# Column term by GpSimd, row terms moved into the feed-forward, and a new order of loads in a cross-attention and feed-forward kernel

## The chip, the cores and the metric

The kernel runs on one core of one Trainium2 chip. The metric is device time in microseconds. Each of the five engines (TensorE for matmuls, VectorE, ScalarE, GpSimd, SyncE) runs its own queue of instructions in order; they wait for each other by semaphores.
## The reference

```python
# x (2, 1024, 2048), ctx (2, 2048, 2048), kernel (2048, 2048), all float32
def fake_quant(x, scale, zp):
    q = jnp.clip(jnp.round(x / scale + zp), 0, 255)
    return (q - zp) * scale

def _layernorm(x): return (x - mean(x)) / sqrt(var(x) + 1e-5)

x = x + fake_quant(_layernorm(x), s1, z1) @ fake_quant(ctx, s2, z2)

y = _layernorm(x)
base = y @ kernel + bias
# the 2 x 1024 tokens are seen as 8 groups of 256; gate (8, 16)
A_eff = einsum('bn,nri->bri', gate, lora_A)      # rank 32
B_eff = einsum('bn,nor->bor', gate, lora_B)
delta = B_eff @ (A_eff @ y) + lora_B_shared @ (lora_A_shared @ y)
x = x + base + delta
```

## The kernel before

A batch (`b` = 0, 1) has 1024 tokens in 8 tiles of 128 (`TILES`) and 2048 columns in 4 blocks of 512 (`NBLK`). For each batch the attention product runs block by block (`first_by_tile`, blocks `j` = 0 to 3), then the feed-forward, again in 4 blocks. Each block's tile `t` has its own PSUM bank `t`. The inner dimension comes in 4 groups `g` (`NG`) of 4 x 128 rows, held in `ring`.

**Attention.** Both operands are quantised to integers. The product uses integers less 127, which are exact in bf16. With q the integer less 127, and d1, d2 the distances of 127 from the zero points, the result is s1*s2*(q1 q2 + d2*sum(q1) + d1*sum(q2) + constant). The part with sum(q1) is the *row term*: one number per token, `RC`. The part with sum(q2) is the *column term*: one number per column, the same for all tokens. TensorE sums each column with one matmul per block into bank 7 (`column_sum`, bank `CB`); ScalarE and VectorE split it into a high and a low half (`column`, `column_low`), and TensorE adds it to each tile with one more matmul (`column_term`, line 1021). The row term is added to x by ScalarE (`row_term`, line 884). `evict1` (VectorE, line 1409) then adds the scaled product to x, which sits in `x2`; it frees the bank for the next block.

Context groups are loaded to `stage`, converted by ScalarE (`conv_ctx`, line 736) and clipped by VectorE (`ctx_group`, line 1362), which also sums them for the column sum (`add_group`).

**Start of batch 0.** x arrives tile by tile (GpSimd's queue); VectorE makes statistics, GpSimd the inverse roots (`root_pair`), ScalarE the quantised rows (`relu_rows`), VectorE the rounding (`round1`). Tiles 0 to 3 are transposed by TensorE (`turn`, `turn_out`), tiles 4 to 7 by DMA (`turn_q`). After block 0 of batch 0, TensorE forms the gated LoRA matrices (`a_effective`, line 1049; `b_effective`, line 1060) from `lora_a`, `lora_b`; they are written out by `store_a_part` and the stores to `bg_scratch`. Their largest values are found with all-reduces over partitions on GpSimd (`largest`, line 588): 1 for A, 2 for B, 3 and 4 for parts of W.

**Feed-forward.** `norm2` normalises a tile; ScalarE takes the high f16 part (`split_hi`), VectorE the low one (`low2`); SyncE transposes each by DMA (`turn_y`, lines 355 and 360). W is split alike (`conv_w` on ScalarE, line 748; `w_group` on VectorE, line 1396). Each step is three matmuls, high by high, high by low, low by high (lines 1154 to 1156). The first block opens with tiles 0 and 1 together (`base0_pair`): group by group, both tiles. LoRA products follow between the tiles (`lora_in`, line 1177; `product_p`). GpSimd adds the bias to x (`add_bias`, line 617), and `evict2` (line 1448) finishes a tile.

The order on each engine is written out by hand; nothing is rearranged by a scheduler.

## Time and profile before

| | us |
|---|---|
| Median of 3 runs | 1066.53 (1066.3 to 1067.35) |
| Profiled execution, its own time | 1063.74 |
| Profiled execution, span from first to last instruction | 1061.7 |
| TensorE busy | 1003.1 (94%), 4791 matmuls |
| VectorE busy | 532.3 (50%) |
| ScalarE busy | 311.5 (29%) |
| GpSimd busy | 163.4 (15%) |
| TensorE's mean granted clock | 0.989 of full |

A busy share says how long an engine computed, not whether anybody waited for it. In rows of the timeline the first number is the start in us, the second the time in us, then engine, line, operation, written tile, read tiles, shape and count; in square brackets stands how long the engine had been idle before it, and what ended that. Engines are written PE (TensorE), DVE (VectorE), ACT (ScalarE), POOL (GpSimd); SPq and POOLq are instructions of the sequencer. Matmul times overlap (a matmul of 0.38 us follows the last one after 0.22 us), so distances are read from starts.

### The profile page before, as it was taken

How to read it: one execution, taken by the hardware profiler on the slowest of the kernel's cores; microseconds unless marked ns; L12 is line 12 of the kernel's file. 1: busy time of each engine (PE TensorE's matmuls, PEld its weight loads, DVE VectorE, ACT ScalarE, POOL GpSimd, SP SyncE). 2: the span in 40 equal slices, each digit the busy share in tenths (PEclk: the TensorE clock that was granted, in tenths of full speed). 3: DMA queues.
4: the chain of work that ended last, by engine and by line, in shares of the span. 5: the costliest groups of instructions: out<-in, count | busy, mean ns of one | idle time of the engine just before them, and what ended most of it. 6: DMA issues, size and time to landing. Idle time of an engine off the chain costs nothing.

```text
span 1061.7 us, 12294 instructions
## 1 busy us (share of the span) xinstructions
PE 1003.1 (94%) x4791; PEld 472.9 (45%) x4791; DVE 532.3 (50%) x764; ACT 311.5 (29%) x266; POOL 163.4 (15%) x199
## 2 busy tenths in 40 slices
PE   2778999799999999999999999999999999999996
PEld 1345444355544444444444444445544444444442
DVE  6754677879655455463423555987632023014010
ACT  4666731322032132232223743532121021003000
POOL 3101100101102211311510000020104004004110
PEclk9989999899999999999999999999999999999998
DMA  8869682767735446338599844456935025004010
GB/s 365 255 192 368 260 346 96 184 139 183 201 127 195 168 149 212 138 112 251 204 299 262 336 179 159 80 166 147 222 110 169 20 80 187 20 30 158 10 42 27
DMA packets 124392, 181.70 MB, mean 171 GB/s; under 512 B 96064, under 2 KB 96064, under 8 KB 111808
## 3 DMA queue, kind: packets, MB, share of 16 engines
q1 hardware_dynamic: 109600, 118.25, 37.3%
q0 software_dynamic: 13600, 58.73, 15.3%
q10 hardware_dynamic: 1152, 4.19, 1.0%
q8 instruction: 25, 0.41, 0.2%
q14 instruction: 15, 0.12, 0.0%
HBM read 128.72 MB, written 29.36 MB: 149 GB/s over the span
## 4 chain that ended last, share of the span: by engine, by line
PE 68%; DVE 11%; DMA 10%; issue 4%; ACT 3%; POOL 1%; SPq 1%; DVEq 0%; POOLq 0%; ACTq 0%
PE psum L1154 16%; PE psum L1156 16%; PE psum L1155 16%; PE psum L987 15%; DMA stage<-in_w 2%; DMA x<-in_x 2%; PE psum L1177 2%; DMA lhs<-in_lora_b 1%; DVE ring L1396 1%; DMA xn<-in_x 1%; DVE stats L1421 1%; DVE hl L1441 1%; DVE stats L1308 1%; DMA bias_sb<-in_bias 1%; DMA lhs<-ap_st 1%
## 5 line engine op out<-in xcount | busy, mean ns | idle before, releaser
L1154 PE MATMUL psum<-ring,lhs 128*128 128x512 f16 x1024 | 388.8, 380 | 9.4 <-DMA lhs<-hl 7.4
L1155 PE MATMUL psum<-ring,lhs 128*128 128x512 f16 x1024 | 388.8, 380 | 0.0
L1156 PE MATMUL psum<-ring,lhs 128*128 128x512 f16 x1024 | 388.8, 380 | 0.0
L987 PE MATMUL psum<-ring,lhs 128*128 128x512 bf16 x1024 | 235.2, 386 | 9.0 <-DMA lhs<-ap_st 7.1
L987 PEld LDWEIGHTS psum<-ring,lhs 128*128 128x128 bf16 x1024 | 101.4, 99 | 134.8 <-issue 15.4
L1154 PEld LDWEIGHTS psum<-ring,lhs 128*128 128x128 f16 x1024 | 100.3, 98 | 132.3 <-issue 10.1
L1156 PEld LDWEIGHTS psum<-ring,lhs 128*128 128x128 f16 x1024 | 100.4, 98 | 121.3 <-issue 0.8
L1155 PEld LDWEIGHTS psum<-ring,lhs 128*128 128x128 f16 x1024 | 100.3, 98 | 119.9 <-issue 0.8
L1448 DVE SCALAR_TENSOR_TENSOR x<-psum,sc,x 128x512 f32<-128x512 f32 (+1 forms) x64 | 45.3, 746 | 182.2 <-PE psum L1166 181.4
L748 ACT ACTIVATE ring<-stage,sc 128x2048 f16<-128x2048 f32 x32 | 63.7, 2002 | 202.6 <-PE psum L1156 159.4
L617 POOL TENSOR_TENSOR x<-x,bias_sb 128x512 f32<-128x512 f32 (+1 forms) x64 | 87.7, 1396 | 173.5 <-DVE xn L1431 98.2
L1396 DVE SCALAR_TENSOR_TENSOR ring<-stage,sc,ring 128x2048 f16<-128x2048 f32 x32 | 75.7, 2376 | 76.4 <-ACT ring L748 76.2
L736 ACT ACTIVATE ring<-stage,pats_sb,sc 128x2048 int16<-128x2048 f32 x30 | 62.3, 2092 | 75.4 <-DMA stage<-in_ctx_in 37.8
L623 POOL DMA_DIRECT2D out<-x x48 | 26.7, 556 | 241.6 <-DVE x L1448 237.8
L1409 DVE SCALAR_TENSOR_TENSOR x<-psum,sc,x 128x512 f32<-128x512 f32 x64 | 45.6, 746 | 34.8 <-PE psum L1021 33.7
L724 ACT ACTIVATE hl<-xn 128x2048 f16<-128x2048 f32 x16 | 30.6, 1912 | 67.6 <-DVE xn L1431 63.0
L1362 DVE TENSOR_SCALAR ring<-ring 128x2048 bf16<-128x2048 int16 x30 | 20.7, 691 | 58.4 <-ACT ring L736 58.4
L1402 DVE SCALAR_TENSOR_TENSOR b_st<-stage,sc,b_st 64x1024 f16<-64x1024 f32 x16 | 21.6, 1350 | 47.9 <-ACT b_st L755 47.8
L1281 DVE BATCH_NORM_STATS2 stats<-xn 128x6 f32<-128x512 f32 x32 | 19.8, 682 | 47.2 <-DMA xn<-in_x 47.1
L1441 DVE TENSOR_TENSOR hl<-xn,hl 128x2048 f16<-128x2048 f32 x16 | 36.7, 2292 | 4.6 <-DMA lhs<-hl 4.4
L884 ACT ACTIVATE x<-x,sc 128x512 f32<-128x512 f32 (+1 forms) x48 | 37.2, 855 | 0.4 <-DVE sc L1350 0.4
L755 ACT ACTIVATE b_st<-stage,sc 128x1024 f16<-128x1024 f32 x16 | 18.4, 1150 | 63.8 <-DMA stage<-in_lora_bs 63.8
(158 smaller groups left out, 644.9 us busy)
## 6 DMA issues: line engine op xcount, KB each, us to landing
stage<-in_w SPq DMA_DIRECT2D x38, 1024.0 KB, 6.0
stage<-in_ctx_in SPq DMA_DIRECT2D x30, 1024.0 KB, 7.9
out<-x POOLq DMA_DIRECT2D x64, 256.0 KB, 3.5
x<-in_x POOLq DMA_DIRECT2D x8, 1024.0 KB, 11.9
xn<-in_x POOLq DMA_DIRECT2D x8, 1024.0 KB, 7.3
x<-in_x POOLq DMA_DIRECT2D x4, 2048.0 KB, 15.9
lhs<-in_lora_a POOLq DMA_DIRECT2D x4, 1024.0 KB, 6.9
lhs<-in_lora_b SPq DMA_DIRECT2D x4, 1024.0 KB, 13.3
```

The lines of the kernel that those rows point to most:

```text
L617: pool.tensor_tensor(v, v, bias_sb[:, :], ALU.add).then_inc(biased, 1)
L736: act.activation(ring_i[:, g, j % 2, :, :], stage[:, i % 2, :, :], ACT.Relu, bias=Z2, scale=IS2).then_inc(act_conv, 1)
L748: act.activation(ring[:, g, 0, :, :], stage[:, i % 2, :, :], ACT.Copy, scale=of_block(CW0, j)).then_inc(act_conv, 1)
L884: act.activation(v, v, ACT.Identity, bias=RC[:, t:t + 1]).then_inc(with_row, 1)
L987: last = pe.matmul(psum[:, t, :], lhs_q[:, k, t * P:(t + 1) * P], ring_q[:, g, j % 2, u, :], start=(k == 0), stop=False)
L1154: pe.matmul(psum[:, t, :], hi, ring[:, g, 0, u, :], start=(kk == 0), stop=False)
L1155: pe.matmul(psum[:, t, :], hi, ring[:, g, 1, u, :], start=False, stop=False)
L1156: last = pe.matmul(psum[:, t, :], lo, ring[:, g, 0, u, :], start=False, stop=False)
L1396: dve.scalar_tensor_tensor(out=ring[:, g, 1, :, :], in0=stage[:, half_w(b, g), :, :], scalar=of_block(CW0, j), in1=ring[:, g, 0, :, :], op ...
L1409: dve.scalar_tensor_tensor(out=v, in0=psum[:, t, :], scalar=S12, in1=v, op0=ALU.mult, op1=ALU.add).then_inc(evicted, 1)
L1441: dve.tensor_tensor(hl[:, 1, :], xn[:, :], hl[:, 0, :], ALU.subtract).then_inc(y_lo, 1)
L1448: dve.scalar_tensor_tensor(out=v, in0=psum[:, t, :], scalar=of_block(INVS0, j), in1=v, op0=ALU.mult, op1=ALU.add).then_inc(evicted, 1)
```

## The change

It has six parts.

1. **Column term.** Block 0 of batch 0 stays as it was. From block 1 on, ScalarE writes the whole column term in f32 to `bias_sb` (`column`, semaphore `col_row`), GpSimd adds it to each tile of x (`add_column`, semaphore `with_col`), `evict1` waits for `with_col`, and TensorE's `column_term` and VectorE's `column_low` are gone from these blocks. The adds stand in GpSimd's queue between the all-reduces and the stores of A.
2. **Row terms.** They leave the attention blocks; ScalarE adds them to a whole tile (2048 columns) in the feed-forward, after the tile has been normalised. A number that is the same over a token's row drops out of its layernorm.
3. **x.** Tiles 4 to 7 are requested together, and LoRA A parts 0 and 1 right after `root_pair(1)`.
4. **Loads on SyncE.** The first two context groups of block 1 follow the transposes of tiles 4 to 7; LoRA B part 1 comes ahead of context group 2, part 3 ahead of group 3; the context of block 2 waits for `be_full` 8.
5. **Orders on VectorE and ScalarE** at the start (rounding of tiles 4 and 5 and their scales earlier), around the LoRA parts (block 0's evictions before `row_terms`, B's copies apart from their maxima), and in the opening of the feed-forward (`w_group(b, 0, 0)` ahead of tile 2's statistics and of `low2(b, 1)`).
6. **Opening.** `base0_pair` starts with tile 0's first group, then takes the high half of tile 1, and asks for tile 1's low half only later.

```diff
@@ gpsimd
-            load_x([4, 5])
+            load_x(range(4, TILES))
             root_pair(1)
-            load_x([6, 7])
...
+            load_lora_a(0)
+            load_lora_a(1)
             root_pair(2)
-            load_lora_a(0)
             root_pair(3)
-            load_lora_a(1)
...
+            def add_column(b, j, tiles=range(TILES)):
+                pool.wait_ge(col_row, b * NBLK + j)
+                if b:
+                    pool.wait_ge(res_in[j], 16)
+                for t in tiles:
+                    if b == 0:
+                        pool.wait_ge(relued, t + 1)
+                    v = x2[:, t, j * NW:(j + 1) * NW]
+                    pool.tensor_tensor(v, v, bias_sb[:, :], ALU.add).then_inc(with_col, 1)
...
                     largest(1, MX_A, PW_A)
+                    add_column(b, 1, range(2))
                     largest(2, MX_B, PW_B)
-                    store_a(b)
-                    largest(3, MX_W, PW_W)
+                    add_column(b, 1, range(2, TILES))
                 else:
                     load_residual(b, NBLK - 1)
-                    store_a(b)
+                    add_column(b, 0)
+                    add_column(b, 1)
+                store_a(b, [0, 1])
+                add_column(b, 2)
+                store_a(b, [2, 3])
+                add_column(b, 3, [0])
+                if b == 0:
+                    largest(3, MX_W, PW_W)
+                add_column(b, 3, range(1, TILES))
                 add_bias(b, 0, blk2(b, 0), False)
@@ sync
             load_ctx(0, 0, [0, 1])
-            load_ctx(0, 1, [0, 1])
             for t in range(PT, TILES):
                 turn_q(t)
+            load_ctx(0, 1, [0, 1])
...
             load_lora_b(0)
+            load_lora_b(1)
             load_ctx(0, 1, [2])
-            load_lora_b(1)
-            load_ctx(0, 1, [3])
             load_lora_b(2)
             load_lora_b(3)
+            load_ctx(0, 1, [3])
+            sp.wait_ge(be_full, 8)
             load_ctx(0, 2, [0, 1])
...
                         turn_y(b, 0)
-                        turn_y(b, 1)
+                        turn_high(b, 1)
+                    if g == 2 and isinstance(j, int) and j == 0:
+                        turn_low(b, 1)
@@ scalar
+                    if n == 0:
+                        act.activation(col_parts, psum[:, CB, :], ACT.Copy, scale=D1).then_inc(col_hi, 1)
+                    else:
+                        if n > 1:
+                            act.wait_ge(with_col, (n - 1) * TILES)
+                        act.activation(bias_sb[:, :], psum[:, CB, :], ACT.Copy, scale=D1F).then_inc(col_row, 1)
+                def row_term(t):
+                    act.wait_ge(rows_ready, b + 1)
+                    act.activation(x2[:, t, :], x2[:, t, :], ACT.Identity, bias=RC[:, t:t + 1]).then_inc(with_row, 1)
@@ vector
             def evict1(b, j, t):
                 dve.wait_ge(psum_full, blk(b, 0, j) * TILES + t + 1)
-                dve.wait_ge(with_row, (2 + j) * TILES + t + 1 if b else min(j, 1) * TILES + t + 1)
+                if b or j:
+                    dve.wait_ge(with_col, (b * NBLK + j - 1) * TILES + t + 1)
...
                 evict1(b, j, 3)
-                early_stats2(b, 2)
-                late_stats2(b, 2)
+                w_group(b, 0, 0)
                 low2(b, 1)
                 evict1(b, j, 4)
                 evict1(b, j, 5)
-                w_group(b, 0, 0)
                 w_group(b, 0, 1)
                 evict1(b, j, 6)
                 evict1(b, j, 7)
                 w_group(b, 0, 2)
+                stats2(b, 2)
                 w_group(b, 0, 3)
@@ tensor, base0_pair
+                    tile_in(0)
+                    bank_free(k, 0)
+                    pe.wait_ge(converted, grp_w(b, 0, 0) + 1)
+                    base_group(0, 0)
+                    high_in(1)
+                    bank_free(k, 1)
+                    high_group(1, 0)
+                    pe.wait_ge(converted, grp_w(b, 0, 1) + 1)
+                    base_group(0, 1)
+                    low_in(1)
+                    low_group(1, 0)
+                    base_group(1, 1)
```

GpSimd's queue in batch 0, from the stores of the LoRA B parts to the first bias add, before. A row of these lists has the line, the operation, written and read tiles, and the semaphores it waits for; the all-reduces are the rows `ISA sc<-sc`, and a bare `ISA` ahead of them or of an add is a MODIFY_POOL_CONFIG.

```order
L634 DMA bg_scratch<-hl 128x2x512 [waits be_dve,be_act] x2
L588 ISA
L588 ISA sc<-sc 128x1 [waits red_in] x2
L600 DMA a_scratch<-lhs 128x2048 [waits a_lo] x4
L588 ISA sc<-sc 128x1 [waits red_in]
L610 DMA bias_sb<-in_bias 128x512 [waits psum_full]
L617 ISA
L617 TENSOR_TENSOR x<-x,bias_sb 128x512 [waits normed2,bias_in]
```

The same queue after, up to the end of block 1's adds:

```order
L656 DMA bg_scratch<-hl 128x2x512 [waits be_dve,be_act] x2
L599 ISA
L599 ISA sc<-sc 128x1 [waits red_in]
L616 ISA
L616 TENSOR_TENSOR x<-x,bias_sb 128x512 [waits relued,col_row]
L616 TENSOR_TENSOR x<-x,bias_sb 128x512 [waits relued]
L599 ISA
L599 ISA sc<-sc 128x1 [waits red_in]
L616 ISA
L616 TENSOR_TENSOR x<-x,bias_sb 128x512 [waits relued,col_row]
L616 TENSOR_TENSOR x<-x,bias_sb 128x512 [waits relued] x5
```

Two all-reduces in a row have become all-reduce, two adds, all-reduce, six adds. In block 3 the queue after has one add, `L599 ISA`, the all-reduce, `L616 ISA`, and seven adds.

VectorE's queue in block 1 of batch 0, before, from block 2's context group 1 to its group 3 (line 1409 evicts block 1; lines 1555 and 1562 make low parts of LoRA A; 1362 clips a context group):

```order
L1409 SCALAR_TENSOR_TENSOR x<-psum,sc,x 128x512 [waits with_row,psum_full] x4
L1555 SCALAR_TENSOR_TENSOR lhs<-b_st,sc,lhs 128x16x32 [waits a_hi]
L1562 SCALAR_TENSOR_TENSOR lhs<-lhs,sc 128x16x32 [waits a_hi] x2
L1362 TENSOR_SCALAR ring<-ring 128x2048 [waits act_conv]
L1382 TENSOR_TENSOR xn<-xn,ring 128x2048 [waits grouped,converted]
L1409 SCALAR_TENSOR_TENSOR x<-psum,sc,x 128x512 [waits with_row,psum_full] x2
```

and after:

```order
L1463 SCALAR_TENSOR_TENSOR x<-psum,sc,x 128x512 [waits with_col,psum_full] x4
L1615 SCALAR_TENSOR_TENSOR lhs<-b_st,sc,lhs 128x16x32 [waits a_hi]
L1622 SCALAR_TENSOR_TENSOR lhs<-lhs,sc 128x16x32 [waits a_hi] x2
L1415 TENSOR_SCALAR ring<-ring 128x2048 [waits act_conv]
L1435 TENSOR_TENSOR xn<-xn,ring 128x2048 [waits grouped,converted]
L1463 SCALAR_TENSOR_TENSOR x<-psum,sc,x 128x512 [waits with_col,psum_full] x2
```

The order is the same; the evictions wait for GpSimd's adds in place of ScalarE's row terms, and the context groups stand behind them.

## Rows read from the trace of the kernel before

**Rows 1.** Waits of TensorE: us in total, times, longest.
```profile
PE psum L1154 <- DMA lhs<-hl: 7.4, 2, 6.2
PE psum L987 <- DMA lhs<-ap_st: 7.1, 1, 7.1
PE psum L1060 <- DMA lhs<-in_lora_b: 4.6, 2, 3.2
```

**Rows 2.** Timeline of TensorE, batch 0: start, time, instruction.
```profile
58.58 5.77 PE L987 MATMUL psum<-ring,lhs 128*128 128x512 bf16 x16 [7.05 <-DMA lhs<-ap_st]
...
76.27 14.40 PE L1049 MATMUL psum<-pats_sb,lhs 128*128 128x64 f32 x128
...
129.24 0.38 PE L1021 MATMUL psum<-bias_sb,ones 128*128 128x512 f16 x1
129.46 3.62 PE L987 MATMUL psum<-ring,lhs 128*128 128x512 bf16 x16
...
143.92 0.38 PE L1007 MATMUL psum<-xn,ones 128*128 128x512 f16 x1
...
170.03 3.62 PE L987 MATMUL psum<-ring,lhs 128*128 128x512 bf16 x16
```

**Rows 3.** Timeline of VectorE, GpSimd and SyncE's queue, 46 to 60 us.
```profile
46.58 0.69 DVE L1337 TENSOR_SCALAR ap_st<-ap_st 128x2048 bf16<-128x2048 int16 x1
...
47.80 0.56 POOL L565 DMA_DIRECT2D lhs<-in_lora_a  x1
...
47.29 10.74 SPq L350 DMA_TRANSPOSE lhs<-ap_st  x2
58.07 4.83 SPq L350 DMA_TRANSPOSE lhs<-ring  x2
```

**Rows 4.** Timeline of ScalarE, 98 to 104 us.
```profile
98.97 2.10 ACT L736 ACTIVATE ring<-stage,pats_sb,sc 128x2048 int16<-128x2048 f32 x1 [4.43 <-DMA stage<-in_ctx_in]
...
101.92 1.57 ACT L884 ACTIVATE x<-x,sc 128x1536 f32<-128x1536 f32 x1
```

**Rows 5.** GpSimd's code changes and what followed them, from four stretches.
```profile
L588 POOLq MODIFY_POOL_CONFIG  x2: 42/42/42, 114.0 to 114.0; - x2
120.34 0.72 POOL L588 PARTITION_ALL_REDUCE sc<-sc  x2 [6.33 <-issue]
...
L617 POOLq MODIFY_POOL_CONFIG  x2: 37/37/37, 200.7 to 200.7; - x2
209.02 2.48 POOL L617 TENSOR_TENSOR x<-x,bias_sb 128x512 f32<-128x512 f32 x2 [8.39 <-issue]
...
L617 POOLq MODIFY_POOL_CONFIG  x2: 11/11/11, 332.6 to 332.7; - x2
339.90 9.85 POOL L617 TENSOR_TENSOR x<-x,bias_sb 128x512 f32 x8 [18.27 <-issue]
...
L617 POOLq MODIFY_POOL_CONFIG  x2: 37/37/37, 493.3 to 493.4; - x2
505.75 12.27 POOL L617 TENSOR_TENSOR x<-x,bias_sb 128x512 f32<-128x512 f32 x8 [12.48 <-issue]
```

**Rows 6.** Timeline of VectorE, batch 0, blocks 1 and 3.
```profile
128.18 2.73 DVE L1409 SCALAR_TENSOR_TENSOR x<-psum,sc,x 128x512 f32<-128x512 f32 x4
...
140.67 0.75 DVE L1409 SCALAR_TENSOR_TENSOR x<-psum,sc,x 128x512 f32<-128x512 f32 x1 [0.22 <-PE psum L1021]
...
187.94 0.74 DVE L1409 SCALAR_TENSOR_TENSOR x<-psum,sc,x 128x512 f32<-128x512 f32 x1
...
214.41 2.35 DVE L1396 SCALAR_TENSOR_TENSOR ring<-stage,sc,ring 128x2048 f16<-128x2048 f32 x1 [0.53 <-ACT ring L748]
```

**Rows 7.** TensorE and SyncE's queue in the opening of batch 1.
```profile
691.00 0.38 PE L1154 MATMUL psum<-ring,lhs 128*128 128x512 f16 x1 [1.24 <-DMA lhs<-hl]
...
710.84 1.82 SPq L360 DMA_TRANSPOSE lhs<-hl  x1
```

**Rows 8.** Timeline of VectorE at 697 us.
```profile
696.92 3.18 DVE L1396 SCALAR_TENSOR_TENSOR ring<-stage,sc,ring 128x2048 f16<-128x2048 f32 x1 [3.36 <-ACT ring L748]
```

More of the change, by code:

```diff
@@ L594, in load_residual, with store_a @@
                                x_tok[b][:, :, j * NW:(j + 1) * NW]).then_inc(res_in[j], 16)
-            def store_a(b):
-                for g in range(GPB):
+            def add_column(b, j, tiles=range(TILES)):
[7 more added lines that the diff above has]
+                    pool.tensor_tensor(v, v, bias_sb[:, :], ALU.add).then_inc(with_col, 1)
+            def store_a(b, gs):
+                for g in gs:
                     pool.wait_ge(a_lo, b * (GPB + 1) + g + 2)
@@ L879, in column @@
                         act.wait_ge(biased, b * NBLK * TILES)
-                    act.activation(col_parts[:, n % 2, :], psum[:, CB, :], ACT.Copy, scale=D1).then_inc(col_hi, 1)
-                def row_term(t, first, last):
-                    v = x2[:, t, first * NW:last * NW]
-                    act.activation(v, v, ACT.Identity, bias=RC[:, t:t + 1]).then_inc(with_row, 1)
-                def row_terms(first, last):
-                    for t in range(TILES):
-                        row_term(t, first, last)
+                    if n == 0:
[7 more added lines that the diff above has]
+                    act.activation(x2[:, t, :], x2[:, t, :], ACT.Identity, bias=RC[:, t:t + 1]).then_inc(with_row, 1)
                 if b == 0:
@@ L895, in _ @@
                         sum_rows(t)
-                    act.wait_ge(rows_ready, b + 1)
-                    for t in range(TILES):
-                        row_term(t, 0, 1)
                     for c in range(NBLK):
@@ L987, in group1 @@
                     last = pe.matmul(psum[:, t, :], lhs_q[:, k, t * P:(t + 1) * P], ring_q[:, g, j % 2, u, :],
-                                     start=(k == 0), stop=False)
-                if g < NG - 1 and t == TILES - 1:
+                                     start=(k == 0), stop=(k == KT - 1 and not by_pe))
+                if g == NG - 1 and not by_pe:
+                    last.then_inc(psum_full, 1)
+                elif g < NG - 1 and t == TILES - 1:
                     last.then_inc(ring_free, 1)
@@ L1014, in column_sum, with column_term @@
                     last.then_inc(csum_full, 1)
-            def column_term(b, j, tiles):
-                n = b * NBLK + j
-                pe.wait_ge(col_ready, n + 1)
+            def column_term(tiles):
+                pe.wait_ge(col_ready, 1)
                 for t in tiles:
-                    pe.matmul(psum[:, t, :], ones[:, :], col_parts[:, n % 2, :], start=False, stop=True).then_inc(psum_full, 1)
+                    pe.matmul(psum[:, t, :], ones[:, :], col_parts, start=False, stop=True).then_inc(psum_full, 1)
             def tile_start(b, j, t):
@@ L1034, in tile_start @@
                 bank_free(blk(b, 0, j), t)
+                if t == CB and (b or j):
+                    pe.wait_ge(col_row, b * NBLK + j)
                 if b == 0 and j == 1:
@@ L1102, in first_block @@
                     for g in range(NG):
-                        group1(0, t, g)
-                    column_term(0, 0, range(t + 1) if t == PT else [t])
+                        group1(0, t, g, True)
+                    column_term(range(t + 1) if t == PT else [t])
                 for c in range(NBLK):
@@ L1120, in first_by_tile @@
                         column_sum(b, j)
-                    first = 1 if tail else TILES // 2 - 1
-                    if t >= first:
-                        column_term(b, j, range(t + 1) if t == first else [t])
                 if tail:
@@ L1129, in first_by_tile @@
                             group1(j, t, g)
-                    column_term(b, j, range(TILES - tail, TILES))
             def base(b, t, j, k, gi):
@@ L1146, in last_bases, with high_group, low_group @@
                         base_group(t, g)
+            def high_group(t, g):
+                for u in range(GU):
+                    kk = g * GU + u
+                    hi = lhs[:, 0, kk, t * P:(t + 1) * P]
+                    pe.matmul(psum[:, t, :], hi, ring[:, g, 0, u, :], start=(kk == 0), stop=False)
+                    pe.matmul(psum[:, t, :], hi, ring[:, g, 1, u, :], start=False, stop=False)
+            def low_group(t, g):
+                for u in range(GU):
+                    lo = lhs[:, 1, g * GU + u, t * P:(t + 1) * P]
+                    pe.matmul(psum[:, t, :], lo, ring[:, g, 0, u, :], start=False, stop=False)
             def base_group(t, g):
@@ L1186, in _, with high_in, low_in @@
                 k = blk(b, 1, 0)
+                def high_in(t):
+                    pe.wait_ge(turned[0], turns2(b, t, 0))
+                def low_in(t):
+                    pe.wait_ge(turned[1], turns2(b, t, 1))
                 def tile_in(t):
-                    pe.wait_ge(turned[0], turns2(b, t, 0))
-                    pe.wait_ge(turned[1], turns2(b, t, 1))
+                    high_in(t)
+                    low_in(t)
                 def base0_pair():
-                    for t in range(2):
-                        tile_in(t)
-                        bank_free(k, t)
-                    for g in range(NG):
+                    tile_in(0)
[10 more added lines that the diff above has]
+                    base_group(1, 1)
+                    for g in range(2, NG):
                         pe.wait_ge(converted, grp_w(b, 0, g) + 1)
@@ L1481, in evict_and_convert @@
                     peak_a(1)
+                    peak_a(2)
                     ctx_group(b, j + 1, 2)
-                    peak_a(2)
+                    peak_a(3)
+                    for c in range(NBLK - 1):
+                        copy_b(c)
                     ctx_group(b, j + 1, 3)
+                    copy_b(NBLK - 1)
                     return
```

81 lines of the change are left out of this document (42 added, 39 removed).

## The prediction

> **What bounds the kernel now.** I read the waits of TensorE first, then its timeline, then the queues that it waits for. TensorE computes for 94% of the span; its idle time lies in a few places. It waits 7.1 us at the start for the first transposed token tile (tile 4), 4.6 us for LoRA B, and 7.4 us where the two feed-forwards open [rows 1]. Elsewhere it streams, and there one 512-column matmul costs 0.22 us (129.24 to 129.46, [rows 2]). So what leaves its queue is worth its length only where nothing else is late. In the openings VectorE's queue decides: from 187.94 to the end of the W group at 214.41 it works nearly without a gap [rows 6].
>
> **Start.** LoRA A part 1 was requested at 47.80, between two transposes; both transposes hold SyncE's queue for 10.74 us, the next two, alone, for 4.83 [rows 3]. After the change all of x and LoRA A 0 and 1 are requested by about 25 us and the context groups of block 1 wait behind the transposes, so the same bytes are through by about 39. Rounding of tile 4 stood at 46.58 [rows 3]; with its scales moved ahead of a head group and of tile 6's statistics I get 42.1 (2.47 us of statistics and about 2 us of queue less), and with a 4.6 us transpose it is there at 47, before TensorE has finished its column sum. Gone: the 7.05 us wait, and the slow matmuls behind it (the 16 at 58.58 took 5.77 us, 16 at full clock 3.45: 2.3 us). The transposes by TensorE come 0.6 us sooner. Against that the column's halves are ready only at 55.4 (ScalarE has relu 6 and 7 first): 1.1 us of wait. Sum 7.05 + 2.3 + 0.6 - 1.1 = 8.8 us; LoRA A's matmuls start at 67.5, not 76.27 [rows 2]. If the transposes are slow by themselves this gives only 5; if LoRA A part 2 also falls beside tile 7's, little changes, as tile 7 has 5 us to spare.
>
> **LoRA B.** Four parts of LoRA B, two context groups and four half-size stores went through between 82 and 105: 8 units, 2.9 us each. The last context group reached ScalarE at 98.97 [rows 4]. Now it is last of its six; 8 units from 73.3 end at about 96. Then conversion 2.1, clip and sums 3.1, the last B copy 0.7, the last store's issue 0.8: GpSimd is done with its stores at 102.6, not 114.0. TensorE's 4.6 us [rows 1] go, but it stands 1 to 2 us for the last copy.
>
> **Column term.** 56 matmuls of 0.216 us leave TensorE: 12.1 us, 24 of them (5.2) in batch 0 and 32 (6.9) in batch 1. In their place GpSimd adds a full row to x, tile by tile, 1.27 us each (209.02: two in 2.48, [rows 5]), and every eviction from block 1 on waits for it. Behind such an eviction stand, in VectorE's queue, the two last context groups of the next block; TensorE waits for those in its tile 0 and for eviction 7 at its column sum.
>
> GpSimd changes its code between the all-reduce and the add, and the trace has the price: from MODIFY_POOL_CONFIG to the next instruction 114.0 to 120.34 (6.3), 200.7 to 209.02 (8.3), 332.7 to 339.90 (7.2), 493.4 to 505.75 (12.3) [rows 5]. Before, one such change stood between the stores and the end of block 3, and nobody waited. After, the order is all-reduce, 2 adds, all-reduce, 6 adds in block 1 (four changes), and add, all-reduce, 7 adds in block 3 (two). I take 8.3 for the first, which falls into busy DMA as the one at 200.7 did, and 7.2 for the rest; bounds are 6.3 and 12.3.
> The Trainium skill (GPSIMD Engine Reference, Instruction dispatch) puts the first call after such a load at about 6 us and says to budget for it; the trace is above it each time. By it the six changes would cost 35.7 us, not 8.3 + 5 x 7.2 = 44.3, and the sum would be 8.6 us less.
>
> Block 1: 102.6 + 8.3 + 0.4 + 7.2 + 2.5 + 7.2 + 0.4 + 7.2 + 1.3 = 137.1 for the row in tile 2. From eviction 2 to the end of eviction 7 VectorE has the work that now runs from 128.18 to 141.4 [rows 6], less two evictions and a wait: 12.8 us. Column sum of block 2: 149.9, against 143.92 [rows 2]. TensorE, whose block 1 ends near 126, stands for about 22 us, and starts cold (2.3 us, as at 58.58). Seven tiles of 3.456 follow: block 3 starts at 176.6, not 170.03 [rows 2]. The 8.8 us of the start and the matmuls of block 1 are spent.
> Block 3: column sum after 3.7 us, ScalarE 0.8, add 1.3, change 7.2, all-reduce 0.4, change 7.2, add 1.3: tile 1 can be evicted at 198.5, not 187.94. From there to the end of the fourth W group VectorE has 25.5 us of work (evictions, one tile's late statistics, two low parts, four W groups, tile 2's statistics, one norm): 224.0 against 216.8 [rows 6]: 7.2 us late. TensorE itself opens sooner relative to VectorE, half by half, and ends its pair only some 4 us late, but tile 2 and the sums of the LoRA product, which it already waits for, follow VectorE. **Batch 0: +7.2 us.**
>
> **Batch 1.** No all-reduce, so no code change. Block 0's adds start once the residual of block 3 is requested, near 588; TensorE needs the first only at 599 and eviction 7 at 602.6, against 601.7: hidden, by 0.9 us. ScalarE is rid of its row terms per block, hidden too; the eight long ones (2048 columns, so about 2.1 us by the 1.57 of 1536, [rows 4]) fit beside its other 2.1 us of each 7.3 us tile. TensorE reaches the opening 6.9 us sooner and the 1.24 us wait at 691.00 [rows 7] goes, since tile 1's low part is asked for only after tile 0's group: 8.1 us. But tile 2's low part, turned by SyncE at 710.84 [rows 7], comes only 6.7 us sooner (four W groups and tile 2's statistics in a row on VectorE), and TensorE stands 1.4 us for it. **Batch 1: -6.7 us.** While GpSimd adds, VectorE is slower: a W group took 3.18 us at 696.92 [rows 8] against 2.35 at 214.41 [rows 6]; VectorE waits for a ring slot there anyway, so I add nothing.
> The row terms that leave batch 0's blocks lay beside matmuls but for 1.3 us before block 1's column parts; TensorE's new stand swallows that. The order in which SyncE asks for W, and for the low part of tile 1, gives 0 to 1 us, in the above.
>
> **Sum.** +7.2 - 6.7 = +0.5 us on the profiled 1063.74 (its span 1061.7, and 2.0 around it). The median shown is 1066.53, 2.8 above; so 1067.0.
>
> **Rivals.**
> A, cheap changes (faster). If each change takes 6.3 as at 114.0, 2.0 + 5 x 0.9 = 6.5 us go: 1060.5. For it: two of the four in block 1 find quiet DMA. Against: 332.7 had quiet DMA too and took 7.2. The page's 6 us belongs here: by its own figure 1058.4. Chance 0.25.
> B, dear changes (slower). All six are in series with TensorE. If busy DMA (W, context and gates are all asked for between 96 and 118) makes the first 12.3 and the others 8.3, that is 4.0 + 5 x 1.1 = 9.5 us: 1076.5. It decides from 0.45 us more per change on. Chance 0.2.
> C, the start gives less (slower). If transposes stay at 10.7 us and LoRA B is no sooner, the stores end 4 to 9 us later and all of batch 0 with them: 1071 to 1076. For it: no trace shows a transpose at that time alone. Chance 0.08.
> D, no code change between add and all-reduce: block 1's 22 us stand is gone, about 1037. Against: every pass in the loops shows it. Chance 0.03.
>
> **Numbers.** The forecast (cancelling within 4 us either way) has 0.44: 0.22 of it within 0.2% (2.1 us, about what timing of this kernel can tell from no change), 0.11 on either side. Faster: 0.11 + 0.25 + 0.03 = 0.39; same: 0.22 and 0.02 from the edges of B and C, 0.24; slower 0.37. The range takes A's 1060.5 and most of B's, 1059.5 to 1075; the forecast's own is 1063 to 1071.
>
> **What would show it.** Right: no TensorE wait near 51 to 58; six code changes on GpSimd between the B stores and the bias, 6 to 12 us each; one TensorE stand of some 22 us in block 2's tile 0, ended by VectorE's context groups and eviction; first feed-forward opening near 209; the second without a wait, then about 1.4 us at tile 2. Wrong: a stand under 10 us in block 2, or a transpose wait at the start; either moves the total by as much.

## The result, and the profile after

| | before | changed |
|---|---|---|
| Median of 6 runs, us | 1066.41 (1064.5 to 1067.56) | 1076.05 (1071.13 to 1083.03) |
| Profiled execution, its own time | 1063.74 | 1083.03 |
| Span | 1061.7 | 1081.5 |
| TensorE's mean granted clock | 0.989 | 0.978 |
| First matmul of LoRA A | 76.27 | 67.06 |
| Column sum of batch 0, block 1 / 2 / 3 | 112.92 / 143.92 / 173.49 | 101.53 / 153.90 / 184.68 |
| First attention matmul of batch 1 | 571.32 | 587.98 |
| Column sum of batch 1, block 0 / 1 | 581.68 / 604.34 | 598.12 / 625.26 |
| First matmul of the second opening | 691.00 | 708.11 |
| End of TensorE's work | 1052.65 | 1072.42 |

The change makes the kernel slower: ratio 1.0099, 95% interval 1.0059 to 1.0138. The forecast was 1067.0, no clear change, with a range to 1075; the median is 9.0 us above the forecast and 1 us above the range. The profiled execution is the slowest of the six, 7 us above their median, so its losses are larger than those of a usual run.

Some of TensorE's waits in the changed kernel (us in total, times, longest), beside [rows 1]. The long wait at the very start (15.2 us, 15.0 before) is left out:

```profile
PE psum L1010 <- DVE ring L1415: 25.1, 6, 19.1
PE psum L1190 <- DVE ring L1449: 8.2, 4, 3.8
PE psum L1190 <- issue: 6.1, 5, 1.9
PE psum L1201 <- DVE ap_st L1517: 5.8, 3, 2.9
PE psum L1032 <- DVE x L1463: 3.9, 2, 2.0
PE psum L1086 <- DMA lhs<-in_lora_b: 0.7, 1, 0.7
```

The waits for transposed tiles and nearly all of the wait for LoRA B are gone. In their place stands one wait of 19.1 us for a context group of VectorE. The rows of lines 1190 and 1201 lie in the feed-forward. Before, they came to 1.6, 0.3 and 3.2 us; the kernel below with the column term back on TensorE has 1.5, 5.2 and 5.3 us. So the waits for `ap_st` and for "issue" do not come from the column term.

GpSimd's timeline in the changed kernel, batch 0, beside [rows 5]:

```profile
101.95 0.73 POOL L656 DMA_DIRECT2D bg_scratch<-hl  x1 [7.11 <-DVE hl L1585]
111.39 0.38 POOL L599 PARTITION_ALL_REDUCE sc<-sc  x1 [8.71 <-issue]
121.48 2.49 POOL L616 TENSOR_TENSOR x<-x,bias_sb 128x512 f32<-128x512 f32 x2 [9.72 <-issue]
129.82 0.38 POOL L599 PARTITION_ALL_REDUCE sc<-sc  x1 [5.85 <-issue]
136.93 8.71 POOL L616 TENSOR_TENSOR x<-x,bias_sb 128x512 f32<-128x512 f32 x6 [6.72 <-issue]
...
193.08 0.38 POOL L599 PARTITION_ALL_REDUCE sc<-sc  x1 [5.94 <-issue]
200.25 10.44 POOL L616 TENSOR_TENSOR x<-x,bias_sb 128x512 f32<-128x512 f32 x6 [6.79 <-issue]
```

Six code changes, each read as the idle time that "issue" ended: 8.71 + 9.72 + 5.85 + 6.72 + 5.94 + 6.79 = 43.7 us. The Trainium skill (GPSIMD Engine Reference, Instruction dispatch) gives about 6 us for such a load. Two of the six agree (5.85 and 5.94), two take 6.7 to 6.8, and the first two 8.7 and 9.7. A view by stretches shows what else differs (the stretch, its length, busy times of TensorE, its weight loads, VectorE, ScalarE and GpSimd, then the granted clock, DMA share, GB/s):

```profile
102.70:111.40 8.70, 8.65 (x41) 3.93 (x41) 7.36 (x9) 4.19 (x2) 0.01 (x1) 1.00 1.02 397
111.80:121.50 9.70, 9.65 (x46) 4.38 (x45) 0.79 (x5) 6.53 (x6) 0.01 (x1) 1.00 0.96 383
124.00:129.80 5.80, 3.81 (x18) 1.54 (x16) 0.75 (x1) 1.68 (x1) 0.00 (x0) 1.00 0.07 31
130.20:136.90 6.70, 0.00 (x0) 0.00 (x0) 0.00 (x0) 0.00 (x0) 0.00 (x1) 0.68 0.00 0
187.20:193.00 5.80, 5.75 (x28) 2.65 (x27) 3.88 (x9) 0.20 (x1) 0.00 (x0) 1.00 0.00 0
193.50:200.20 6.70, 6.70 (x32) 3.04 (x31) 5.19 (x16) 1.06 (x1) 0.00 (x0) 1.00 0.01 2
```

The two long ones fall where the DMA engines are full (shares 1.02 and 0.96); the four with shares of 0.07 or less take 5.85 to 6.79. No run changed the DMA load alone, so that the load is the cause is not shown.

VectorE in block 1 of batch 0, beside [rows 6]:

```profile
138.28 0.75 DVE L1463 SCALAR_TENSOR_TENSOR x<-psum,sc,x 128x512 f32<-128x512 f32 x1 [13.45 <-POOL x L616]
140.18 2.67 DVE L1615 SCALAR_TENSOR_TENSOR lhs<-b_st,sc,lhs 128x512 f16<-128x512 f32 x2
142.78 3.41 DVE L1622 SCALAR_TENSOR_TENSOR lhs<-lhs,sc 128x512 f16<-128x512 f32 x2
146.11 0.70 DVE L1415 TENSOR_SCALAR ring<-ring 128x2048 bf16<-128x2048 int16 x1
```

The eviction of tile 2 waits 13.45 us for GpSimd. Behind it the low parts of LoRA A (lines 1615 and 1622), two in 2.67 and two in 3.41 us, run beside the adds; without full-width adds beside them each pair takes 1.40 or 1.41 us, as two kernels show below. What TensorE does meanwhile:

```profile
146.87 1.89 PE L1010 MATMUL psum<-ring,lhs 128*128 128x512 bf16 x4 [19.06 <-DVE ring L1415]
150.04 1.89 PE L1010 MATMUL psum<-ring,lhs 128*128 128x512 bf16 x4 [1.29 <-DVE ring L1415]
153.90 0.59 PE L1032 MATMUL psum<-xn,ones 128*128 128x512 f16 x1 [1.96 <-DVE x L1463]
```

It stands 19.06 us, and four matmuls then take 1.89 us. The view by stretches gives the granted clock there:

```profile
146.00:158.00 12.00, 7.66 (x17) 2.37 (x19) 11.76 (x14) 2.67 (x2) 3.57 (x4) 0.50 0.28 104
```

The clock is 0.50, the 1.2 GHz level, right after the stand. In batch 1 there is no code change, and still there is a new loss. VectorE and GpSimd at 603 us:

```profile
603.47 11.46 DVE L1435 TENSOR_TENSOR xn<-ring 128x2048 f16<-128x2048 bf16 x1
614.86 2.71 DVE L1463 SCALAR_TENSOR_TENSOR x<-psum,sc,x 128x512 f32<-128x512 f32 x4
```

```profile
603.09 0.91 POOL L604 DMA_DIRECT2D x<-in_x  x1 [8.38 <-DMA out<-x]
604.01 9.84 POOL L616 TENSOR_TENSOR x<-x,bias_sb 128x512 f32<-128x512 f32 x8
```

Before, the same sum had this row:

```profile
586.82 1.23 DVE L1382 TENSOR_TENSOR xn<-ring 128x2048 f16<-128x2048 bf16 x1
```

The instruction that begins 0.54 us ahead of the first of eight adds ends 1.1 us after the last. The adds themselves come 16 us after the batch's first attention matmul, because the request for the last residual (line 604) waits for stored outputs and stands ahead of them. Before, that request stood at nearly the same distance from the batch's first attention matmul (586.87 against 571.32, 15.6 us):

```profile
586.87 0.91 POOL L593 DMA_DIRECT2D x<-in_x  x1 [8.61 <-DMA out<-x]
```

Behind the held instruction the evictions are late, and TensorE waits in block 1 of batch 1:

```profile
618.23 1.04 PE L1010 MATMUL psum<-ring,lhs 128*128 128x512 bf16 x4 [0.68 <-DVE ring L1415]
621.40 1.89 PE L1010 MATMUL psum<-ring,lhs 128*128 128x512 bf16 x4 [2.14 <-DVE ring L1415]
625.26 0.58 PE L1032 MATMUL psum<-xn,ones 128*128 128x512 f16 x1 [1.96 <-DVE x L1463]
```

### The profile page after: what moved, and what is told of

Read it like the earlier page. It is cut to its first block, busy times and chain, and to the rows that moved or that the text cites. A ratio compares the mean times of both kernels' runs of the same rounds, so it can differ in the third digit from the quotient of the medians.

```text
span 1081.5 us, 12196 instructions
## 1 busy us (share of the span) xinstructions
PE 996.2 (92%) x4713; PEld 467.8 (43%) x4735; DVE 549.8 (51%) x758; ACT 305.7 (28%) x234; POOL 247.3 (23%) x255
## 4 chain that ended last, share of the span: by engine, by line
PE 63%; DVE 11%; issue 10%; DMA 7%; ACT 4%; POOL 2%; SPq 1%; DVEq 0%; POOLq 0%; ACTq 0%
PE psum L1190 15%; PE psum L1191 15%; PE psum L1192 15%; PE psum L1010 11%; DMA stage<-in_w 2%; PE psum L1213 2%; PE psum L1075 1%; DMA stage<-in_ctx_in 1%; DMA bias_sb<-in_bias 1%; POOL x L616 1%; DVE ring L1449 1%; DMA xn<-in_x 1%; DVE x L1463 1%; PE psum L1201 1%; ACT ring L778 1%
## 5 line engine op out<-in xcount | busy, mean ns | idle before, releaser
L616 POOL TENSOR_TENSOR x<-x,bias_sb 128x512 f32<-128x512 f32 x56 | 83.3, 1518 | 68.7 <-ACT bias_sb L915 45.5
L1415 DVE TENSOR_SCALAR ring<-ring 128x2048 bf16<-128x2048 int16 x30 | 23.8, 796 | 51.5 <-ACT ring L766 51.4
```

Of the source, the lines that this page charges most:

```text
L616: pool.tensor_tensor(v, v, bias_sb[:, :], ALU.add).then_inc(with_col, 1)
```

## The experiments

My theory after the result: in batch 0 the code changes stand in series with TensorE as forecast, and in both batches the adds slow VectorE down, which was priced at nothing. Rivals: the changes are harmless and the adds' own time is the cost; or the moved row terms or the new opening cost the time. All times are medians; each kernel was timed beside the kernel before, whose median was 1065.93 in the first group, 1066.77 in the second, 1067.3 in the third and 1065.86 in the last.

**No code changes.** (Maxima over partitions are left out.)

```diff
-                pool.partition_all_reduce(dst, src, P, RED.max).then_inc(red_out, 1)
+                if n < 4:
+                    pool.tensor_tensor(dst, src, ONE, ALU.mult).then_inc(red_out, 1)
+                else:
+                    pool.partition_all_reduce(dst, src, P, RED.max).then_inc(red_out, 1)
```

> The changed kernel, but the three all-reduces of blocks 1 to 3 of batch 0 (largest 1, 2, 3) are replaced by a multiplication by one on GpSimd: the maxima over partitions are left out, and with them the six code changes. Theory (code changes in series with the evictions, 43.8 us in the profiled run): the row for tile 2 stands by 115 us, not 138.28; TensorE's stand in block 2 goes; column sum of block 2 near 131, not 153.90; eviction (3,1) near 178, not 201.62; median 1050 to 1056, some 22 us under the changed kernel and 10 or more under the kernel before. Rival (the adds themselves and their contention with VectorE cost the time): less than 8 us less than the changed kernel, and a stand remains in block 2.

Measured 1048.79 (ratio 0.9844, 0.9811 to 0.9877), 27 us under the changed kernel and 1 us under the expected range. Column sum of block 2 at 128.93, no wait for a context group over 2.1 us, and the granted clock from 100 to 230 us is 0.99, not 0.89. So the changes carry the cost in batch 0: with the adds in place and the changes gone, the stand is gone. The rival falls. In batch 1 the held sum is there again, 11.67 us:

```profile
574.08 11.67 DVE L1438 TENSOR_TENSOR xn<-ring 128x2048 f16<-128x2048 bf16 x1
```

**Two changes less.**

```diff
                     largest(1, MX_A, PW_A)
-                    add_column(b, 1, range(2))
                     largest(2, MX_B, PW_B)
-                    add_column(b, 1, range(2, TILES))
+                    add_column(b, 1)
```

> The changed kernel with the all-reduces 1 and 2 together ahead of all eight adds of block 1: four code changes in batch 0 up to the opening, not six. Theory: the peaks of B were ready at 107.5, so both reduces run at 111.4 and the adds start near 120; row for tile 2 near 124.5 in place of 138.28, block 2's column sum near 141 in place of 153.90; median 1062 to 1066 (12 to 13 us less), about as fast as the kernel before. Rival (changes are not in series with TensorE): within 3 us of the changed kernel.

Measured 1063.69 (1059.17 to 1070.68; ratio 1.0002, 0.9979 to 1.0025), 12.4 us less than the changed kernel. GpSimd:

```profile
111.67 0.72 POOL L599 PARTITION_ALL_REDUCE sc<-sc  x2 [9.00 <-issue]
120.95 11.18 POOL L616 TENSOR_TENSOR x<-x,bias_sb 128x512 f32<-128x512 f32 x8 [8.56 <-issue]
```

Column sum of block 2 at 140.39, 13.5 sooner; the two changes saved were 5.85 + 6.72 = 12.6 in the changed kernel. Each of these two changes cost TensorE its full length. Here the context sum of batch 1 began 0.82 us ahead of the adds and took its normal 1.22 us:

```profile
587.67 1.22 DVE L1434 TENSOR_TENSOR xn<-ring 128x2048 f16<-128x2048 bf16 x1
```

The eight adds took 11.57 us, not the 9.84 of the changed kernel, where VectorE was held beside them; here VectorE worked beside them, and its sums took up to 2.18 us. The adds began as late as in the changed kernel (16.2 us after the batch's first attention matmul), at full width and back to back, but nothing was held, and the column sums of blocks (1,0) and (1,1) lie 21.9 us apart, not 27.1. With narrow adds, below, they lie 20.9 apart. So late adds of full width cost about 1 us here when nothing is held, and about 6 when something is.

**Adds behind TensorE's tiles.**

```diff
+                    elif t:
+                        pool.wait_ge(psum_full, blk(b, 0, j) * TILES + t)
```

> The changed kernel, but in batch 1 GpSimd adds the row to tile t only once TensorE has finished tile t-1 of that block, so the adds never run back to back beside VectorE's context sums. Theory (eight adds in a row hold VectorE up): the context sum at 603.47, 11.46 us there, takes 1.2 to 2.5 us; the waits of 0.68 + 2.14 + 1.96 us in block (1,1) go; 4 to 8 us less than the changed kernel, 1068 to 1072, and less spread between runs. Rival (the slow sum is off TensorE's path or is hidden elsewhere): same time within 2 us. Second rival (the added wait delays the evictions): slower by 1 to 4 us.

Measured 1077.74 (1076.79 to 1078.2; ratio 1.0121, 1.0096 to 1.0145), no gain: the theory's number failed, and the time is the first rival's. The trace shows a part of the reason. The adds of block (1,0) were so late that the added wait never bound them; they ran in a row from 603.77 to 613.6, and a clip of VectorE was held in their midst:

```profile
609.50 4.69 DVE L1417 TENSOR_SCALAR ring<-ring 128x2048 bf16<-128x2048 int16 x1
```

The first attention matmul of batch 1 to its opening took 115.8 us, against 120.1 in the profiled execution of the changed kernel, so a shorter hold did give time back in the trace; but the column sum of block 2 came 1.7 us later than there, and the medians show no gain. A late start is what left the added wait without effect here.

**The column term back on TensorE**, in all blocks, with everything else changed.

```diff
+        BY_PE = 8      # columns 0..7: column_term on TensorE, column_low on VectorE, no add_column
```

> The changed kernel with its column term back on TensorE in all eight blocks (72 more... that is 56 more matmuls of 0.216 us), and the high and low halves back on ScalarE and VectorE; start, load order, row terms in the feed-forward and opening half by half stay. Theory: the start's 9.2 us and LoRA B's 2.4 us are kept through block 2, batch 0's opening gives 3 to 4 us more, batch 1's 1 to 2; median 1048 to 1054. Rival (the row terms in the feed-forward, or the new opening, cost time): 1058 or more.

Measured 1053.15 (ratio 0.9897, 0.9872 to 0.9922), as expected. So the column term by GpSimd costs the change 21 us by the ratios and 23 by the medians.

**The start alone.**

```diff
-            load_x([4, 5])
+            load_x(range(4, TILES))
...
-            load_ctx(0, 1, [0, 1])
             for t in range(PT, TILES):
                 turn_q(t)
+            load_ctx(0, 1, [0, 1])
...
```

> The kernel before with the start alone changed: all of x and LoRA A 0 and 1 requested early, the load order of context and LoRA B, and the orders on VectorE and ScalarE around them; column term, row terms and opening as before. Theory: LoRA A's matmuls start near 67 in place of 76.27, block 1's column sum near 101.5 in place of 112.92, and nothing gives it back: 11 to 12 us less than before, 1054 to 1056. That would leave 1 to 2 us for opening and row terms together in the kernel with the column on TensorE. Rival (VectorE's queue in the opening takes it back, as it decides there): 1059 to 1063.

Measured 1053.6 (ratio 0.9886, 0.9856 to 0.9917): the start gives 12 to 13 us, slightly more than expected, and nothing takes it back. LoRA A begins at 66.9, block 1's column sum is at 101.53.

**Column term split**: TensorE in batch 0, GpSimd in batch 1.

```diff
+        BY_PE = 4
```

> The changed kernel with the column term on TensorE in batch 0 and by GpSimd in batch 1 as changed: adds of block (1,0) behind the request for the residual of block 3, back to back. Theory: 32 matmuls of 0.216 us leave batch 1, 6.9 us, and up to 6 us come back where a context sum of VectorE is held behind the eight adds; 1046 without that, 1052 with it, and runs spread by more than 4 us. Rival (GpSimd's adds in batch 1 cost as much as they save whatever their order): 1053 or more in all runs.

Measured 1055.18 (1052.03 to 1061.53; ratio 0.988, 0.9855 to 0.9905). The spread is as the theory had it, the times are not: they were to lie between 1046 and 1052, and three of the four runs are above 1055, where the rival had them. 6.9 us of matmuls are gone and the time is that of the kernel with all of the column term on TensorE, within 2 us either way. The profiled run, the slowest, has the held instruction again, and it is another one, a clip:

```profile
581.01 10.41 DVE L1431 TENSOR_SCALAR ring<-ring 128x2048 bf16<-128x2048 int16 x1 [3.25 <-ACT ring L772]
```

```profile
581.05 9.82 POOL L619 TENSOR_TENSOR x<-x,bias_sb 128x512 f32<-128x512 f32 x8
```

Column sums of blocks (1,0) and (1,1) lie 27.9 us apart. In batch 0, with no adds beside them, the low parts take:

```profile
115.65 1.41 DVE L1634 SCALAR_TENSOR_TENSOR lhs<-b_st,sc,lhs 128x512 f16<-128x512 f32 x2
116.97 1.41 DVE L1641 SCALAR_TENSOR_TENSOR lhs<-lhs,sc 128x512 f16<-128x512 f32 x2
```

(These two rows are of "Split, order alone", below, whose batch 0 is the same.)

**Split, adds early and spaced.**

```diff
-                    load_residual(b, NBLK - 1)
                     add_column(b, 0)
+                    load_residual(b, NBLK - 1)
```

with the spacing of "Adds behind TensorE's tiles".

> As column_split, but in batch 1 the adds of block 0 come ahead of the request for the residual of block 3 (which waits for the last outputs of batch 0 to be stored), and each add waits for TensorE's previous tile. Theory: the adds start near 4 us sooner and are spaced, the evictions of block (1,0) are in time, no sum on VectorE takes over 5 us; distance of the column sums of blocks (1,0) and (1,1) 20.9 to 22 us (27.1 in the changed kernel); 1045 to 1048, spread under 3 us. Rival (a held instruction does not depend on the order): as column_split.

Measured 1048.41 (1046.38 to 1053.0; ratio 0.982, 0.9797 to 0.9843), the lowest median here, 1.8% under the kernel before and 0.4 us above the expected range. The spread of 6.6 us was wider than the expected 3. Column sums 574.59 and 595.52, 20.9 apart; no VectorE instruction with its operands in SBUF took longer than 2.18 us beside the adds of block (1,0):

```profile
585.72 2.18 DVE L1453 TENSOR_TENSOR xn<-xn,ring 128x2048 f16<-128x2048 f16 x1
```

**Narrow adds.** (The column term is left out of 448 of 512 columns.)

```diff
-                    v = x2[:, t, j * NW:(j + 1) * NW]
-                    pool.tensor_tensor(v, v, bias_sb[:, :], ALU.add).then_inc(with_col, 1)
+                    v = x2[:, t, j * NW:j * NW + 64]
+                    pool.tensor_tensor(v, v, bias_sb[:, 0:64], ALU.add).then_inc(with_col, 1)
```

> The changed kernel, but GpSimd adds the column term to 64 of the 512 columns of each tile; the other columns go without it. All waits and all code changes stay, the adds take about 0.2 us each and hardly touch the memory. Theory (code changes cost what the forecast said, the rest of the miss is the adds' contention with VectorE): column sum of block 2 near 148 in place of 153.90 (2.5 us of add time and 4 of slowed VectorE), VectorE's W groups at 2.35 us, no held sum in batch 1; 10 to 14 us less than the changed kernel, 1062 to 1066. Rival (the adds are harmless, the miss is elsewhere): at most 4 us less, 1072 or more.

Measured 1065.57 (ratio 0.9994, 0.9973 to 1.0014), 10.5 less than the changed kernel by the medians, 11.2 by the ratios. Column sum of block 2 at 147.33. The low parts of LoRA A, with the same work and the same order as in the changed kernel (2.67 and 3.41 us there), now take:

```profile
136.91 1.40 DVE L1615 SCALAR_TENSOR_TENSOR lhs<-b_st,sc,lhs 128x512 f16<-128x512 f32 x2
138.23 1.41 DVE L1622 SCALAR_TENSOR_TENSOR lhs<-lhs,sc 128x512 f16<-128x512 f32 x2
```

From the eviction of tile 2 to the column sum of block 2 it takes 11.75 us (from 135.58), against 15.62 us in the changed kernel (from 138.28): 3.9 us by contention with the adds. In batch 1 nothing is held, and from its first attention matmul to the opening it takes 111.37 us; before it took 119.68, in the changed kernel's profiled run 120.13. The rival falls. The adds still come late here, at 596.36, 16.9 us after the batch's first attention matmul, and TensorE does not wait: being late does no harm by itself.

**All by GpSimd, mended**: merged reduces, all-reduce 3 ahead of all adds of block 3, early and spaced adds in batch 1.

> The changed kernel with three changes of order: all-reduces 1 and 2 together ahead of block 1's adds; all-reduce 3 ahead of all adds of block 3; in batch 1 the adds of block 0 ahead of the request for the last residual, each add behind TensorE's previous tile. The column term stays with GpSimd from block 1 on. Theory: merging gives the 12 us that it gave alone; the third all-reduce earlier lets eviction (3,1) go 4 to 6 us sooner relative to the column sum of block 3 (31.6 us from block 3's column sum of the kernel with merged reduces is not needed for this: 16.9 us there in the changed kernel, 11 to 13 expected); batch 1 gives 3 to 5 us. Sum 1052 to 1058. Rival (the W sum comes too late for the earlier place, or the opening is bound by VectorE's work anyway): 1060 or more.

Measured 1065.63 (ratio 0.9988, 0.9971 to 1.0005): the theory's number failed and the rival's held, though for another reason. The all-reduce came sooner, but now the first eviction of block 3 waits for the add behind two changes:

```profile
182.38 0.75 DVE L1463 SCALAR_TENSOR_TENSOR x<-psum,sc,x 128x512 f32<-128x512 f32 x1 [6.37 <-POOL x L618]
```

TensorE's first wait for a product's half stands at 281.58, against 277.55 with merged reduces alone. That this eviction is all that was lost is not shown. Batch 1 took 111.15 us up to its opening, the distance it has with nothing held, so that part of the theory held.

**Opening undone**, on top of the kernel with the column term back on TensorE: `base0_pair`, the order of the low halves and VectorE's order as before.

> The kernel with the column on TensorE and the new start, row terms in the feed-forward, but the opening of the feed-forward as before (both tiles of a pair together, tile 2's statistics ahead of the W groups). It tells the opening from the row terms, which together came to 0 to 1 us (1053.15 with both, 1053.6 with neither). Theory: both are near zero, since TensorE later waits for the second LoRA product and W in any case: 1052 to 1056. Rival (one gains what the other loses): 1050 or less, or 1057 or more.

Measured 1055.0 (ratio 0.9888, 0.9853 to 0.9923). With opening and row terms 1053.15, with row terms 1055.0, with neither 1053.6 (ratios 0.9897, 0.9888 and 0.9886): each is within what these runs can tell from nothing.

**Split, order alone**: as "Split, adds early and spaced", without the spacing.

> As column_split (TensorE adds the column term in batch 0, GpSimd in batch 1), with the adds of block (1,0) ahead of the request for the last residual, but not spaced. Theory: starting 4 to 5 us sooner is what counts, since the evictions then have slack; a VectorE instruction may still be held for up to 10 us, but it costs TensorE at most 2 us: 1047 to 1051. Rival (spacing is what counts): 1052 or more, or a spread over 6 us, as in column_split.

Measured 1050.02 (1049.74 to 1051.31; ratio 0.9844, 0.981 to 0.9878). Column sums 20.9 apart, no VectorE instruction over 2.2 us beside the adds (line 1451 at 579.12, 2.17). Most of what the early, spaced version gains is in the order; the spacing may add 1 to 2 us, within the error. The rival (spacing is what counts) falls.

**Gaps between late adds.**

```diff
+                    elif t > 1:
+                        pool.wait_ge(evicted, blk(b, 0, j) * TILES + t - 1)
```

> As column_split (adds of block (1,0) late, behind the request for the last residual), but in batch 1 the add of tile t waits until VectorE has evicted tile t-2 of that block: no more than two adds stand back to back before VectorE gets a turn. Theory (a held VectorE instruction is released at the first gap in GpSimd's adds): no VectorE instruction in block (1,0) takes over 4 us, where one took 10.41 in column_split; the column sums of (1,0) and (1,1) lie 21 to 23.5 us apart, not 27.9; 1049 to 1052, spread under 4 us. Rival (the hold lasts 10 us by itself, or hits at random): an instruction of 10 us again, 1053 or more and runs up to 1061.

Measured 1051.82 (1049.08 to 1056.76; ratio 0.9875, 0.9840 to 0.9911), with a spread of 7.7 us where under 4 was expected. No VectorE instruction of block (1,0) took over 2.3 us; column sums 22.7 apart. It agrees with the theory, but does not prove it: in this execution the sum ended at 575.8, ahead of the first add at 575.98, so the collision of the other runs was not met. The added wait did not break up the first adds either; six ran in a row until 583.39, and a clip begun at 581.70 took 2.25 us, until just behind the sixth.

## Why the prediction was wrong

**The step that failed** is the price of contention: "While GpSimd adds, VectorE is slower: ... VectorE waits for a ring slot there anyway, so I add nothing." The prediction had seen the slowing (3.18 us against 2.35), dismissed it for one place, and never applied it to the other places where the adds now run. The runs show what stood in its place:
- In block 1 of batch 0 contention cost 3.9 us (11.75 us with narrow adds, 15.62 with full ones), 3.3 of it in lines 1615 and 1622 (6.1 us for four instead of 2.8).
- In batch 1 a VectorE instruction was held for 10 to 12 us. The prediction had "Block 0's adds start ... near 588 ... eviction 7 at 602.6, against 601.7: hidden, by 0.9 us". On the clock of the kernel before, 588 is 16.7 us after the batch's first attention matmul; the adds came at 16.0, so the start was right. Eviction 7 was to be over at 30.4 us on the same count and was over at 37.1. From column sum (1,0) to (1,1) it took 27.1 us against 20.9 with nothing in the way, and 2.8 more in the next block. A margin of 0.9 us had no room for a held instruction.
- With adds of 64 columns the kernel is 10.5 to 11.2 us faster. As an estimate, some 5 us of that is the time of the adds themselves: three in block 1 and two in block 3 stand in the forecast's chain, and each took 0.3 us there, not 1.25. About 6 us are left for contention, of a miss of 9.0.

**The other 3 us are open.** They are within the error: the interval of the changed kernel's ratio is 4 us wide on either side. Two terms were also too small in the traces:
- In block 3 the stretch from eviction (3,1) to the end of the fourth W group took 28.1 us, not 25.5 (201.62 to 229.73). This is hardly contention: with narrow adds it took 27.5, because VectorE then waited 2.8 us for ScalarE's conversions of W, which the forecast left out (1.0 us in the changed kernel).
- From the end of the fourth W group to the first attention matmul of batch 1 it took 358.3 us (358.8 with narrow adds), against 354.6 before; the forecast had no change. One trace cannot settle that: five kernels here have the same batch 0 (the column term on TensorE in it), and from its opening to batch 1 they took between 371.5 and 377.9 us.

By the medians of the other kernels, each against the 1066 us beside it: start alone -13; opening and row terms 0; column term in batch 1 by GpSimd about 0 (+2.0 by the medians, -1.8 by the ratios) where -6.9 was expected; column term in batch 0 +21 to +23 where the forecast's steps make +18.6 (7.2, and the 11.4 of the start that it spent). This way, too, the larger part of the miss is batch 1, with 2 to 4 us in batch 0. The profiled execution, with batch 0 at +16.7 and batch 1 at +3.1, shows more of both; how often the held instruction occurs in the other five runs is not known, since only one was traced. Of the six traces here with late adds of full width in batch 1, three have it. Also open is why some kernels spread by 5 to 8 us without a held instruction in their trace (the kernel before: 1062.1 to 1068.8).

**What was right,** some of it by luck:
- The start: LoRA A at 67.06 (forecast 67.5), last B store done at 102.7 (102.6), transposes 4.46 us in SyncE's queue, 1.4 us of wait for the last copy (1 to 2). Alone it gave 13.2 us by the medians.
- The code changes: 43.7 us in six (forecast 44.3). The sum agrees better than its parts: the four of block 1 took 31.0 us, not 29.9, and the two of block 3 took 12.7, not 14.4. Rival A was right for two of them and rival B's direction for the first two. Rival D fell with the traces; without the changes the kernel took 1048.8 us, not D's 1037.
- One stand of TensorE in block 2's tile 0 (19.1 us, forecast about 22), cold clock behind it. The column sum of block 2 with narrow adds, 147.33, is near the forecast's 149.9 less 2.9 us for three shorter adds, 147.0; this is partly luck, as the row for tile 2 came 1.4 us late and the work behind it was 1 us shorter.
- In batch 1 up to the opening: 119.68 - 6.9 - 1.24 = 111.5, and 111.37 with narrow adds, 111.37 with adds early and spaced, 111.16 with the order alone. Behind the opening these three took 2.7, 5.1 and 4.4 us more than before, where the forecast had 1.4.
- TensorE's wait at tile 2 of the second opening: 1.4 forecast, 1.88 found at 734.37. The profile puts it down to "issue", so that it is the forecast's wait is not shown. The first opening began at 212.98, not near 209.

## What to carry to other kernels

Moving an elementwise term from TensorE to GpSimd was paid for three times here: by the change of code on either side of every all-reduce, by VectorE instructions that ran slower beside the adds, and by what GpSimd's queue already waited for ahead of them. Price each VectorE instruction that will run beside GpSimd's by the slowest row of its kind, allow for one that is held over a whole run of adds, and look at what stands ahead of the new work in its queue. Where the term can go to GpSimd, give it a place with slack and without an all-reduce near. With the term in batch 1 alone that was worth 1 to 5 us by the medians (2 to 8 by the ratios) against TensorE doing it all; from block 1 of batch 0 on, it cost 21 to 23.

## What was not expected of the hardware

VectorE's instructions met the adds in three ways.
- Most of those that began while adds were already running took about one add longer: 2.17 in place of 1.23 (line 1435 at 629.73 below). Some clips took longer: 4.69 us in place of 0.69 with adds behind TensorE's tiles, 2.25 us with gaps between the adds (at 581.70). Both ended within 0.6 us of the end of the run of adds.
- One that began just ahead of the first add was held until all eight were over: 11.46, 11.67 and 10.41 us, with 0.54, 0.75 and 0.04 us of lead. With a lead of 0.82 us it was not held. Four meetings do not show where the border lies or that the lead decides.
- Evictions, which read one operand from PSUM, kept their 0.75 us beside adds (line 1483 at 578.57, with gaps between the adds, below).

```profile
629.73 2.17 DVE L1435 TENSOR_TENSOR xn<-ring 128x2048 f16<-128x2048 bf16 x1
```

```profile
578.57 0.75 DVE L1483 SCALAR_TENSOR_TENSOR x<-psum,sc,x 128x512 f32<-128x512 f32 x1 [0.47 <-POOL x L621]
```

The Trainium skill (SBUF — State Buffer, Who interferes with whom) says that a VectorE instruction with two SBUF inputs, or in a 2-port mode, contends with a GpSimd instruction that reads SBUF, and that one with at most one SBUF input, outside such a mode, does not contend. The evictions (0.75 us) and the one-add delays of the sums (2.17 for 1.23) agree with it. The clips read one operand from SBUF and were delayed; whether they ran in a 2-port mode no run here shows. That an instruction is held over a run of eight GpSimd instructions (11.46 us), although it had begun first, is more than that page says. By the Trainium skill's rule the forecast's "I add nothing" would have had a rival: VectorE slowed wherever two-input work stands beside the adds. The runs give its price: 3.9 us in block 1 of batch 0.
